# Decoder stack, its first two steps: first weights split on ScalarE and VectorE, the second group's input and token products taken into the first step, the top choice spread

## What is computed

```python
# x (8, 256, 256), seen by the attention stack as 2 sequences of 1024 tokens
for i in range(4):                                    # DEPTH
    h = layer_norm(x, ln1_g[i], ln1_b[i])
    q, k, v = h @ Wq[i], h @ Wk[i], h @ Wv[i]         # 8 heads of 32
    lo = local_attn(heads 0..3)                       # windows of 128, the previous one too, causal
    go = causal_linear_attn(heads 4..7)               # buckets of 64, softmax(q), elu(k)+1
    x = x + concat(lo, go) @ Wo[i] + bo[i]
    x = x + gelu(layer_norm(x, ln2_g[i], ln2_b[i]) @ W1[i] + b1[i]) @ W2[i] + b2[i]
x = _layernorm(x0 + x)                                # then: + cross attention, _layernorm,
vals, idx = top_k(logits, 32); w = softmax(vals)      # + MLP with weights composed from 32 chosen
W = einsum('k,kir,kro->io', w, A[idx], B[idx])        # of 64 primitives, twice; _layernorm
```

## Time and profile before

| | us |
|---|---|
| median of 3 runs | 1033.41 |
| lowest and highest | 1031.14, 1034.42 |
| the profiled execution | 1031.39 |
| its span | 1029.5 |
| TensorE busy, VectorE, ScalarE, GpSimd | 971.7, 675.7, 562.6, 485.7 |
| mean granted clock of TensorE | 0.981 |

### The profile page before, as it was taken

How to read it: one execution, slowest core, us unless ns; L and a number is a source line. 1 busy time by engine, 2 the same in 40 slices (tenths; PEclk the granted TensorE clock), 3 DMA queues, 4 the chain that set the end, 5 groups by cost and what they waited for, 6 DMA issues and landing times.

```text
span 1029.5 us, 21804 instructions
## 1 busy us (share of the span) xinstructions
PE 971.7 (94%) x8589; PEld 834.5 (81%) x8589; DVE 675.7 (66%) x1454; ACT 562.6 (55%) x1338; POOL 485.7 (47%) x384
## 2 busy tenths in 40 slices
PE   3677999999999999999999999999999999999997
PEld 2555888888888888888888888888897778997887
DVE  3557676767767676776867677686451786676554
ACT  1516665856666585666657576665715433444210
POOL 7315446626774662677366257733416220007441
PEclk9787999999999999999999999999999999999999
DMA  6201000000210001021000002001047695740001
GB/s 196 83 1 41 2 2 17 2 17 1 83 42 1 18 1 17 2 83 42 2 17 2 17 1 83 1 2 48 1 97 178 127 192 96 152 98 1 21 22 42
DMA packets 71532, 47.56 MB, mean 46 GB/s; under 512 B 44463, under 2 KB 68111, under 8 KB 71439
## 3 DMA queue, kind: packets, MB, share of 16 engines
q1 hardware_dynamic: 71439, 46.27, 18.3%
HBM read 44.16 MB, written 2.10 MB: 45 GB/s over the span
## 4 chain that ended last, share of the span: by engine, by line
PE 86%; DVE 3%; SPq 3%; ACT 3%; issue 2%; POOL 2%; DMA 1%; POOLq 0%; DVEq 0%; ACTq 0%
PE F L1267 18%; PE F L1124 17%; PE A L1124 15%; PE A L1358 4%; PE A L1214 4%; PE A L1516 4%; PE A L1172 3%; PE A L1137 2%; PE A L1231 2%; PE F L1137 2%; PE F L1117 1%; PE A L1489 1%; PE A L1117 1%; PE A L1205 1%; PE A L1188 1%
## 5 line engine op out<-in xcount | busy, mean ns | idle before, releaser
L1124 PE MATMUL F<-xt,w 128*128 128x512 f32 x864 | 218.6, 401 | 4.6 <-ACT scratch L1108 3.9
L406 POOL TENSOR_TENSOR ht<-scratch,ht 128x512 fp32r<-128x512 f32 x128 | 175.7, 1391 | 41.6 <-ACT ht L978 39.9
L1124 PEld LDWEIGHTS F<-xt,w 128*128 128x128 f32 x864 | 157.5, 188 | 45.9 <-ACT scratch L1108 7.6
L1267 PE MATMUL F<-w,ht 128*128 128x256 f32 x1536 | 190.7, 283 | 2.0 <-POOL ht L406 2.0
L1267 PEld LDWEIGHTS F<-w,ht 128*128 128x128 f32 x1536 | 184.1, 189 | 7.8 <-issue 4.6
L395 POOL TENSOR_TENSOR rstd<-var,minus_half 128x4 f32<-128x4 f32 x32 | 37.7, 1179 | 202.5 <-DVE var L528 202.2
L975 ACT ACTIVATE scratch<-F,b_now 128x512 f32<-128x512 f32 x128 | 87.6, 684 | 36.2 <-POOL ht L406 18.0
L1124 PE MATMUL A<-wa,xt 128*128 128x512 f32 x384 | 94.4, 402 | 0.3 <-ACT b1c L1066 0.3
L401 POOL TENSOR_TENSOR x<-x,vec_f 128x1024 f32<-128x1024 f32 x16 | 37.9, 2366 | 104.5 <-DVE scratch L541 104.5
L1124 PEld LDWEIGHTS A<-wa,xt 128*128 128x128 f32 x384 | 72.6, 192 | 17.1 <-ACT b1c L1066 0.4
L978 ACT ACTIVATE ht<-scratch 128x512 fp32r<-128x512 f32 x128 | 81.0, 632 | 4.1
(11 more groups left out here) (204 smaller groups left out, 2005.7 us busy)
## 6 DMA issues: line engine op xcount, KB each, us to landing
raw_f<-in_L_attn_W_dram SPq DMA_DIRECT2D x8, 1024.0 KB, 5.7
scratch<-in_L_ffn_fc_B_dram SPq DMA_DIRECT2D x32, 256.0 KB, 4.4
scratch<-in_L_ffn_fc_A_dram SPq DMA_DIRECT2D x32, 256.0 KB, 4.1
x<-in_x_dram SPq DMA_DIRECT2D x4, 512.0 KB, 7.4
raw_f<-in_L_ffn_fc_A_dram SPq DMA_DIRECT2D x32, 64.0 KB, 3.8
scratch<-in_x_dram SPq DMA_DIRECT2D x1, 2048.0 KB, 12.2
raw_f<-in_L_ffn_fc_B_dram SPq DMA_DIRECT2D x32, 64.0 KB, 3.6
out_dram<-x SPq DMA_DIRECT2D x3, 512.0 KB, 2.9
```

What stands on the lines that cost most here:

```text
L406: pool.tensor_tensor(ht[:, 1, m, :], hf[:, m % 2, :], ht[:, 0, m, :].bitcast(F32), ALU.subtract).then_inc(h_lo, 1)
L1124: last = pe.matmul(out, lhs(a, c), rhs(b, c), start=k == 0, stop=k == len(total) - 1)
L1267: last = pe.matmul(F[:, t % 2, 0:D], ht[:, a, c, P * t:P * t + P], w2[:, b, c, :], start=k == 0, stop=k == len(passes) - 1)
```

## The change

- Loads: the attention weights come in three parts with semaphores of their own (q/k columns, token columns, Wo); the logits and the second group's input are issued ahead of Wo. The two bias rows are loaded on their own, and GpSimd's bias addition waits for them. b1 is loaded later.
- The first layer's `wa` is split by ScalarE (hi) and VectorE (lo), first the q/k columns, then the token columns. GpSimd splits `wa` only in layers 1 to 3.
- ScalarE begins with an exponential on a dummy.
- Step 0 is written out: VectorE normalises group 1 before group 0's token products are out; transposes and q/k products of group 1 go into the banks of `F` and stand after group 0's first scores; the token products of group 1 follow group 0's local attention, and group 0's output product comes after them.
- The top choice is cut into `top_start`, `top_choose`, `top_index`, `top_columns`, placed between other work of steps 0 and 1.
- Step 1 is written out on VectorE: residual add of group 0 and LayerNorm moments early, the LayerNorm shift after the maxima of the second scores. On TensorE the first transposes of the MLP's input wait for the last part of the top choice.

```diff
-        def load_a(sp, l, first=False):
-            if not first:
-                sp.wait_ge(wo_ready, l)
+        def load_a(sp, l, which):
+            parts = (((Wq, 0, P, 0), (Wk, 0, P, P)), ((Wv, 0, D, 2 * P), (Wq, P, D, 4 * P), (Wk, P, D, 5 * P)),
+                     ((Wo, 0, D, 6 * P),))[which]
...
+        def load_bias(sp, l, which, n=None):
+            if n is not None:
+                sp.wait_ge(biased[which], n + 1)
+            row = (bo, b2)[which][bass.ds(l, 1)]
+            sp.dma_start((vec_a, vec_f)[which][:, 2, :], row.broadcast_to([P, D])).then_inc(bias_loaded[which], 16)
...
+            load_a(sp, 0, 0)
+            load_a(sp, 0, 1)
             for f, lg in enumerate((fc1_logits, fc2_logits)):
...
+            load_x(1)
+            load_a(sp, 0, 2)
+            load_bias(sp, 0, 0)
+            load_x(2)
+            load_x(3)
             load_w1(sp, 0, first=True)
...
-                load_vec(sp, l + 1, 0, 4 * l + 3)
-                load_vec(sp, l + 1, 1, 4 * l + 3)
+                for which in range(2):
+                    load_vec(sp, l + 1, which, 4 * l + 3)
+                    load_bias(sp, l + 1, which, 4 * l + 3)
                 load_w2(sp, l + 1)
...
@@ GpSimd, start
-            split_wa(pool, 0)
+            pool_rstd(pool, 0, 1)
             pool.wait_ge(zero_ready, 1)
             pool.wait_ge(top_const, 5)
-            pool.wait_ge(wa_ready, 1)
+            pool.wait_ge(qn_done, 1)
             pool_bias(pool, 0, 0, 0)
             split_wo(pool, 0)
+            pool_bias(pool, 0, 1, 1)
             split_w1(pool, 0)
...
@@ VectorE
+            return F[:, c, :] if i == 1 or n == 1 else A[:, 4 + c, :]
...
+            dve.wait_ge(wa0_hi, 1)
+            lo(dve, wa[:, 1, :, 0:2 * P], raw_a[:, :, 0:2 * P], wa[:, 0, :, 0:2 * P]).then_inc(wa_qk_ready, 1)
             dve_xt_lo(dve, 0, 0)
+            for c in range(DC):
+                dve.wait_ge(wa0_hi, 2 + c)
+                last = lo(dve, wa[:, 1, c, 2 * P:6 * P], raw_a[:, c, 2 * P:6 * P], wa[:, 0, c, 2 * P:6 * P])
+            last.then_inc(wa_ready, 1)
+            top_start()
+            mark_loaded(0)
+            mark_loaded(1)
+            ln_scaled(dve, 0, 1, 1, 0)
+            ln_shifted(dve, 0, 1)
+            mark_loaded(2)
+            mark_loaded(3)
...
+            def first_step():
+                dve_features(dve, 0)
+                dve_max(dve, 0, 0)
+                dve_xt_lo(dve, 0, 1)
+                dve_features2(dve, 0)
+                dve_max(dve, 0, 1)
+                dve_ctx(dve, 0)
+                top_choose()
+                dve_prec(dve, 0)
+                dve_lin_lo(dve, 0)
+                dve_pt(dve, 0, 0)
+                dve_pt(dve, 0, 1)
+                top_index()
+                dve_aloc(dve, 0)
+                dve_al_lo(dve, 0)
+            def second_step():
+                dve_features(dve, 1)
+                dve_res1(dve, 0, 0)
+                dve.wait_ge(res1, 2)
+                ln_moments(dve, 1, 0, 0)
+                dve_max(dve, 1, 0)
+                dve_features2(dve, 1)
+                ln_centred(dve, 1, 0, 0, 0)
+                dve_max(dve, 1, 1)
+                ln_shifted(dve, 1, 0)
+                dve_ctx(dve, 1)
+                top_columns()
+                dve_prec(dve, 1)
+                dve_xt_lo(dve, 1, 0)
...
@@ ScalarE
+            act.wait_ge(const_step, 1)
+            act.activation(carrier[:, 1:2], ones[:, :], ACT.Exp)
...
+            act.wait_ge(raw_qk_loaded, 32)
+            act.activation(wa[:, 0, :, 0:2 * P], raw_a[:, :, 0:2 * P], ACT.Copy).then_inc(wa0_hi, 1)
             act_xt_hi(act, 0, 0)
+            act.wait_ge(raw_tok_loaded, 48)
+            for c in range(DC):
+                act.activation(wa[:, 0, c, 2 * P:6 * P], raw_a[:, c, 2 * P:6 * P], ACT.Copy).then_inc(wa0_hi, 1)
...
+                act_features(act, 0)
+                act_xt_hi(act, 0, 1)
+                act_exp(act, 0, 0)
+                act_qnt(act, 0)
+                act.wait_ge(s_psum, 2)
+                act_q(act, 1)
+                act_k(act, 1)
+                act_exp(act, 0, 1)
...
@@ TensorE
+            def first_step():
+                pe_xt(pe, 0, 0)
+                for i in range(2):
+                    pe_qk(pe, 0, 0, i)
+                for t in range(TILES):
+                    pe_tok(pe, 0, t)
+                pe_s(pe, 0, 0)
+                pe_xt(pe, 0, 1)
+                for i in range(2):
+                    pe_qk(pe, 1, 0, i)
+                pe_qnt(pe, 0)
+                pe_s(pe, 0, 1)
+                pe.wait_ge(qnt_out, 1)
+                pe_ctx(pe, 0)
+                pe.wait_ge(ctxn_done, 1)
+                pe_lin(pe, 0)
+                top_k()
...
+                pe_pt(pe, 0, 0)
+                pe_pnorm(pe, 0)
+                pe_pt(pe, 0, 1)
+                pe_pv(pe, 0)
+                for t in range(TILES):
+                    pe_tok(pe, 1, t)
+                pe_wo(pe, 0, 0)
...
                     pe_s(pe, n, 0)
+                    if not tok:
+                        top_columns()
...
                 if mlp:
+                    if not tok:
+                        pe.wait_ge(b1_ready, 1)
+                        pe.wait_ge(top_wcol, 1)
                     if out:
                         pe.wait_ge(res2, RES2_0 + 4 * (n - 1) - 1)
                     pe_xt(pe, 1, n - 1, (0,))
```

## The result

The changed kernel takes **1020.56 us** (median of 4 runs, 1019.83 to 1021.11) against 1032.45 for the kernel before in the same comparison: a ratio of 0.9886, 95% interval 0.9869 to 0.9902. It is faster, by 11.9 us. The forecast was 1013.0 with a range of 1008.5 to 1018.0: the direction was right, the size was not, and the time lies outside the range. The profiled execution took 1020.84 with a span of 1018.9, 10.6 us less than the span before, at the same mean clock, 0.981.

A forecast was written before the change was run, and what follows sets the result against it. TensorE bounds the kernel from 117 us, so only its earlier idle time can be won: 6.6 plus 18.0 less 4.9 gives 19.7 us; 1031.39 less that is 1011.7, plus 1.3 for run spread, 1013.0, range 1008.5 to 1018.0.

The forecast's parts named there:

- Bound and method: TensorE is gapless from 117 us, so only earlier time can be won, and what is won there is kept.
- Part 1: First weights, from start to group 0's token products: earlier LayerNorm, GpSimd's split off the path; 6.6 us gained.
- Part 2: First step, group 0's token products to group 1's: reordered work and the top choice hide in idle time; 18.0 us gained.
- rival (a): TensorE's clock does not hold in part 2 and rises late in part 1: 3.8 us less gain, 1017; chance 0.15.
- Part 3: Second step, group 1's token products to the probabilities' transposes: the new order costs 4.9 us, 22.98 becoming 27.9.
- rival (c): GpSimd and VectorE collide in the second step, centring beside W2's split: 3.1 us lost, 1016; chance 0.09.
- Rivals (d) to (f): First-step overlap does nothing, 1025, 0.05; exposed bias-row loads, 1052, 0.02; change does not do what it says, 1033, 0.01.
- the slower rival: Bias rows loaded on their own delay GpSimd, 39 us if wholly exposed against 19.7 gained: 1052; chance 0.02.

The follow-up runs named there:

- run with the early shift: Changed kernel with the second step's LayerNorm shift and top choice's columns ahead of the second scores' maxima on VectorE: 1016.52 us, ratio 0.9844.
- run with the top choice later: Changed kernel with the top choice's first half after group 0's attention output, TensorE's part between two token products of group 1: 1013.32 us, ratio 0.982.
- run with GpSimd later: Changed kernel with GpSimd's bias addition and splits of Wo and W1 waiting for the top choice's first half, not the q features: 1013.55 us, ratio 0.9811.
- kernel with both moves: Changed kernel with the top choice after group 0's attention output and GpSimd's work released at the exponentials' second half: 1020.38 us, ratio 0.9894.

## Why the prediction missed

**Bound and method: right.** From the third group's token products to 300 us TensorE has no gap, and what was won ahead of them was kept but for 2.1 us, which other executions do not lose.

**Part 1: right.** 6.2 us for 6.6, shown by the run in which GpSimd splits again. The 0.4 lie ahead of the transposes, which start at 10.39 for 9.9: the row ln1_b landed at 6.77 (1.83+4.94 in the chain), where the forecast had 6.3. The terms behind them, as written, add to 2.6 and not to the 2.7 that the forecast took; measured are 2.6.

**Part 2, the failed step.** The sentence was that the first half of the top choice is "some 2 us of tiny instructions" beside 3.34 us of exponentials, "no cost; if it outlasts them, up to 0.5". Two things that stood in the forecast were not put together. It placed GpSimd's bias, Wo and W1 work from the q features on (31.4) to 48, and the top choice beside exponentials that end at 39.1; and it had measured that the same VectorE form takes 1506 ns beside GpSimd and 475 alone. It took the durations of the top choice from the kernel before, where GpSimd was idle at that time (a 64x2 multiplication took 0.15 us), and asked about the collision at the q subtraction, the weight split and the second step, but not here. And it read 1506 against 475 as a factor of 3.2. By that factor 2.2 us would have become 7; it is not a factor. L717 grew sevenfold, since the price is what is left of GpSimd's instruction (they are 1.0 to 2.3 us long here), anew for each instruction that is hit. Eight are hit (two each of L702, L712, L720, and L709 and L717); together they cost 9.7-2.25=7.5 us, and the reciprocal comes 7 us after the exponentials. TensorE had half of the probabilities' transposes to do meanwhile, so that 5.4 us of it reach the end.

In the traces the instructions hit were SCALAR_TENSOR_TENSOR, TENSOR_TENSOR and TENSOR_SCALAR from SBUF to SBUF, and in the run with GpSimd's split a CAST (64x32, 1.00 us for 0.16); not hit were the reductions, the reciprocals, and copies out of PSUM. The Trainium skill, GPSIMD Engine Reference, section Specifications, which the forecast cited, names the forms (two SBUF inputs, or a 2-port mode). How the price is formed stands on another page, which the forecast did not use: SBUF — State Buffer, section SBUF: two separate sides, calls the shared pair of ports "an **exclusive lock**, not a bandwidth split", held by whichever instruction starts first until its end. The traces agree: VectorE waits, 44.15 beside 44.14, 39.01 beside 38.93, and where VectorE's own instruction is long, GpSimd waits in its turn (1.76 us for 1.30, in the last section). Read together with the start times of GpSimd's queue, it gives the missing term.

**Part 2, the clock.** Group 1's q/k products, counted as 3.0 warm, ran at the low level (2.90+1.50 us; granted clock 0.50 from 28 to 31), which makes the +0.8 up to the q transposes; in the run with GpSimd's split the first six took 1.64, and the stretch 13.67 against the 13.8 forecast. At the last exponential the middle of two levels was taken, and the low one held, 1.3 us. The local product then ran warm (-0.5). In sum 1.6 us, of the kind that rival (a) priced at 3.8; it is not the cause of the miss.

**Part 3: right.** Forecast 27.9 from token products to the probabilities' transposes, measured 27.2. The run with the early shift confirms the mechanism: 8.8 for 11.2.

**GpSimd in the second step, rival (c).** Mechanism right, size less: the centring is hit in part (2.76 us for 1.66), the shift fully (4.83), TensorE waits 0.20 us for it. The stretch is 0.9 longer, and not all by this: 0.4 lie between the local attention product and these transposes (91.87 to 95.14, 3.27 us, for 2.90 before), 0.3 in the stretch's first products, at a granted clock of 0.58 (80.7 to 83).

```profile
86.37 2.76 DVE L558 SCALAR_TENSOR_TENSOR scratch<-x,mv,vec_a 128x256 f32<-128x256 f32 x4
...
90.25 4.83 DVE L567 SCALAR_TENSOR_TENSOR scratch<-scratch,rstd,vec_a 128x256 f32<-128x256 f32 x4
95.14 1.09 PE L1238 MATMUL A<-ident,scratch 128*128 128x128 f32 x8 [0.20 <-DVE scratch L567]
```

**Rivals (d) to (f)** did not occur; the bias rows, the slower rival, never stood in the chain. What was missing was a rival of this kind: GpSimd's work, moved out of the start, lands on whatever VectorE does where it is released.

**The account.** 19.7 us forecast on the profile; less 5.4 for the collision, less 1.6 for the clock in the first step, less 2.1 behind the third group, less 0.1 for all other rows together: 10.5, and the profiled executions differ by 1031.39-1020.84=10.55. Shown by runs are the collision and the parts 1 and 3; the low clock is read from traces, and no run changed it; why a load comes late in the weight composition stays open. The medians give the collision 7.0 and 7.1 us (1020.56-1013.55, 1020.38-1013.32), more than the 5.4 that this account reads from the stretch in one trace; the difference is not resolved. Without the collision the kernel measures 1013.55, beside a forecast of 1013.0; that this is so close is in part luck, since the executions of that kernel alone run from 1011.70 to 1015.12.

## What to carry to other kernels

When an edit moves GpSimd's elementwise work, list what VectorE runs in the window where it will now lie, and price each instruction of the forms that are hit at what is left of the GpSimd instruction beside it, not at a factor of its own length. Chains of many tiny instructions suffer most, since each pays that price anew. Releasing that work 8.5 us later, behind the chain, gave 7 us here by the medians.

## What the runs showed of the hardware

- GpSimd loses nothing to VectorE's small instructions: its four low pieces took 1.26 to 1.27 us each on top of the top choice, 1.27 to 1.30 in the run with the top choice later, where they have ended before it. It does lose to a long one. In the run with GpSimd later the first low piece took 1.76 us, the other three 1.29 to 1.30:

```profile
49.39 2.05 POOL L366 TENSOR_TENSOR w<-raw_f,ones 128x512 fp32r<-128x512 f32 x2
50.47 1.51 DVE L572 TENSOR_TENSOR at<-scratch,at 128x512 fp32r<-128x512 f32 x1 [0.70 <-ACT at L1048]
51.38 1.76 POOL L372 TENSOR_TENSOR w<-raw_f,w 128x512 fp32r<-128x512 f32 x1
```

  VectorE's subtraction waits for the end of GpSimd's piece (51.44) and then runs to 51.98; the GpSimd piece that starts meanwhile is about as much longer.
- Whether VectorE is hit is decided by the form of the instruction: 0.28 us for a reduction of 64x128 and 0.15 for a reciprocal amid GpSimd's work, 0.28 and 0.16 with GpSimd still.
- TensorE's granted clock differs at the same place between kernels whose order on TensorE up to there is the same: the first six q/k products of group 1, behind a wait of 2.38 us in either, took 2.90 us in the change (granted clock 0.50 from 28 to 31) and 1.63 in the kernel with both moves (1.00 from 27 to 29). At this place that is 1.3 us that belong to no edit, and the late block above, 7.4 or 6.2 us, is 1.2 more.
- No pause follows the table load: it ends at 9.13, and the copy starts at 9.14. The Trainium skill, ScalarE: Activation LUTs, section What ACT_TABLE_LOAD costs, adds a drain of 1.38 us to the 1.28 of the load. The trace shows 0.01 behind the load, and ahead of it ScalarE had nothing to finish. In the change, ahead of the fourteen loads at L1022 ScalarE idled 0.2 us in all, and the one at 156.19 ends at 157.47 with the exponential at 157.49, so no drain shows on either side.
